# Context keys of a decoder layer: three high-and-low passes instead of plain fp32, in a new order

## The reference

```python
x = _layernorm(x + attn(x, W_Q, W_K, W_V, W_out, b_out))
# cross-attention, with xn = layer_norm(x, ln_w, ln_b) and vg the gathered context rows
q = xn @ Wq * SCALE
kv = vg @ Wkv                  # context: 77 rows of 256 -> keys 512, values 512
k, v = split(kv, 2)
sim = einsum('bthd,btkhd->bthk', q, k) + where(valid, 0, -10000)
out = einsum('bthk,btkhd->bthd', softmax(sim) * valid, v) @ Wout
# feed-forward
h = silu(x @ wg.T) * (x @ wu.T)
out = h @ wd.T
```

## Time and profile before

| | |
|---|---|
| median of three runs | 2188.42 us (2185.69 to 2190.17) |
| the profiled execution's own time | 2187.84 us |
| its span, first to last instruction | 2186.0 us |
| mean granted TensorE clock, of full | 0.992 |
| TensorE busy | 2121.0 us, 97% |
| weight loads busy | 1864.6 us, 85% |
| VectorE, ScalarE, GpSimd busy | 1574.8, 1331.5, 393.2 us |

### The profile page before, as it was taken

The page is one execution under the profiler, slowest core; times in us unless marked ns, Lnnn a source line. Parts: engine busy times, 40 slices in busy tenths (PEclk is TensorE's granted clock), DMA queues, the critical chain, the costliest instruction groups (busy, mean ns, idle before and its releaser), DMA issues.

```text
span 2186.0 us, 55834 instructions
## 1 busy us (share of the span) xinstructions
PE 2121.0 (97%) x18368; PEld 1864.6 (85%) x18368; DVE 1574.8 (72%) x5700; ACT 1331.5 (61%) x3990; POOL 393.2 (18%) x630
## 2 busy tenths in 40 slices
PE   4899999999999999999999999999999999999986
PEld 3688888888888888888888888888888888888875
DVE  3477777777777777777777777777777777777764
ACT  5666666656666656666656666656666656666642
POOL 3211121111112111112111112111112111112111
PEclk9899999999999999999999999999999999999998
DMA  4100000000000000000000000000000000000000
GB/s 133 41 14 15 15 8 17 17 17 11 16 8 17 17 17 10 17 8 17 17 17 10 17 8 17 17 17 10 17 8 17 17 17 10 17 8 17 14 6 10
DMA packets 48599, 38.47 MB, mean 18 GB/s; under 512 B 19504, under 2 KB 46512, under 8 KB 48560
## 3 DMA queue, kind: packets, MB, share of 16 engines
q1 hardware_dynamic: 48560, 37.96, 6.1%
HBM read 29.56 MB, written 8.39 MB: 17 GB/s over the span
## 4 chain that ended last, share of the span: by engine, by line
PE 95%; DVE 1%; ACT 1%; DMA 1%; POOL 1%; issue 1%; SPq 0%; POOLq 0%; DVEq 0%; ACTq 0%
PE gen L375 21%; PE gen L377 18%; PE gen L376 18%; PE s_ps L509 10%; PE z_ps L543 7%; PE pt_ps L522 3%; PE gen L439 3%; PE gen L457 3%; PE gen L470 3%; PE z_ps L545 3%; PE pt_ps L523 3%; PE pt_ps L527 2%; PE gen L466 2%; PE gen L481 1%; PE gen L434 1%
## 5 line engine op out<-in xcount | busy, mean ns | idle before, releaser
L679 ACT ACTIVATE SM<-SM,least 128x128 f32<-128x128 f32 (+1 forms) x1024 | 452.9, 446 | 142.0 <-DVE least L975 141.9
L975 DVE CUSTOM_DVE_ANT_0 SM<-s_ps,causal 128x128 f32<-128x128 f32 (+1 forms) x1024 | 312.5, 352 | 111.3 <-PE s_ps L509 105.6
L615 ACT ACTIVATE PT<-pt_ps 128x512 f32<-128x512 f32 (+1 forms) x512 | 237.7, 485 | 207.8 <-PE pt_ps L523 161.5
L988 DVE TENSOR_SCALAR SM<-SM,total 128x128 f32<-128x128 f32 (+1 forms) x1024 | 274.5, 332 | 9.1
L1157 POOL TENSOR_TENSOR H_lo<-G,H_hi 128x256 fp32r<-128x256 f32 x192 | 142.1, 753 | 620.7 <-ACT H_hi L615 620.7
L509 PE MATMUL s_ps<-KT,QT 64*128 64x128 f32 (+1 forms) x2048 | 238.5, 351 | 4.3 <-DVE least L975 3.5
L1133 POOL TENSOR_TENSOR var<-moments,eps 128x2 f32<-128x2 f32 x96 | 18.7, 195 | 1054.3 <-DVE moments L847 1054.3
L679 ACT ACTIVATION_READ_ACCUMULATOR SM<-SM,least 128x1 f32 x1024 | 195.3, 191 | 0.0
L543 PE MATMUL z_ps<-PT,Vt 128*64 128x256 f32 x1024 | 170.4, 407 | 6.2 <-ACT PT L615 6.2
L509 PEld LDWEIGHTS s_ps<-KT,QT 64*128 64x128 f32 x2048 | 135.0, 187 | 43.2 <-issue 28.6
L984 DVE RECIPROCAL total<-total 128x4 f32<-128x4 f32 x256 | 44.4, 173 | 163.6 <-ACT SM L679 159.3
(11 more groups left out here) (176 smaller groups left out, 6611.8 us busy)
## 6 DMA issues: line engine op xcount, KB each, us to landing
xT_in<-in_xT SPq DMA_DIRECT2D x32, 256.0 KB, 2.8
x_in<-in_x SPq DMA_DIRECT2D x32, 256.0 KB, 2.8
out<-XN SPq DMA_DIRECT2D x32, 256.0 KB, 2.2
ctx_in<-in_ctxT SPq DMA_DIRECT2D x32, 77.0 KB, 2.4
mask_in<-in_maskT SPq DMA_DIRECT2D x32, 77.0 KB, 2.6
QX<-in_wq SPq DMA_DIRECT2D x1, 512.0 KB, 4.6
QP<-in_wq SPq DMA_DIRECT2D x1, 512.0 KB, 5.4
xwk<-in_xwkv SPq DMA_DIRECT2D x1, 512.0 KB, 5.5
```

The costliest lines, as they stand in the source:

```text
L615: return act.activation(o, i, ACT.Copy)
L679: ins = act.activation(part, part, ACT.Exp, scale=-1.0, bias=least[:, i % 2, n:n + 1], accum_out=total[:, i % 2, n:n + 1])
L975: ins = dve.tensor_tensor_reduce(SM[:, i % 2, at:at + keys], s_ps[h][:, t * P:t * P + keys], causal[:, S - keys:S], -SCALE, -3 * NEG, ALU. ...
L988: ins = dve.tensor_scalar(part, part, total[:, i % 2, n:n + 1], None, ALU.mult)
```

## The change

The weights of the context keys become a pair of halves, `xwk_s`, staged like the others and so the first late weight after the out projection; there are 12 late weights in place of 11. The context halves get a 78th column, set to zero once by GpSimd, and the keys are computed by `project` from the halves, 78 columns wide, in 8 blocks of three passes. Of each 78 columns ScalarE copies 77 as before. The keys now wait for `ctx_low` and not for the landing of `ctx_in`, and the next context's transfer waits for `ctx_low` alone. The scratch of dynamic DMAs is set to 4096 bytes. The order of all four engines is written anew.

```diff
-        xwk = sb("xwk", [P, KD, XE])
+        xwk_s = halves("xwk", [P, KD, XE])
...
-        ctx_s = halves("ctxs", [P, KD, V])
+        ctx_s = halves("ctxs", [P, KD, V + 1])
...
-        for w, parts, per in ((wq, wq_s, 1), (wk, wk_s, 2), (wv, wv_s, 2), (wo, wo_s, 4), (xwkv[:, XE:], xwv_s, 2),
+        for w, parts, per in ((wq, wq_s, 1), (wk, wk_s, 2), (wv, wv_s, 2), (wo, wo_s, 4), (xwkv[:, 0:XE], xwk_s, 2),
+                              (xwkv[:, XE:], xwv_s, 2),
...
                     if it.other:
-                        for bank, value in it.read("oXK"):
-                            sp.wait_ge(gen_read[bank], value)
                         sp.wait_ge(ctx_low.sem, ctx_low.at(b, 0))
...
-                    sp.dma_start(xwk[:, :, :], xwkv[:, 0:XE].rearrange("(k p) n -> p k n", p=P)).then_inc(small_in.sem, 16)
...
                     elif kind == "XK":
-                        pe.wait_ge(ctx_loaded.sem, ctx_loaded.at(r, 1))
+                        pe.wait_ge(ctx_low.sem, ctx_low.at(r, 1))
                         for m in range(XP):
-                            for k in range(KD):
-                                ins = pe.matmul(ps[:, m * V:(m + 1) * V], xwk[:, k, m * P:(m + 1) * P],
-                                                ctx_in[:, k, :], start=(k == 0), stop=(k == KD - 1))
+                            ins = project(ps[:, m * (V + 1):(m + 1) * (V + 1)], tile_of(xwk_s, slice(m * P, (m + 1) * P)),
+                                          tile_of(ctx_s, whole), KD)
...
-                fill("oXK")
+                fill("aQ1")
                 scores(0)
-                fill("aQ1")
+                fill("aK1")
...
                 fill("aQ3")
+                transposed("a", 4)
+                values("a", 3)
                 fill("oSIM10")
-                values("a", 3)
                 scores(6)
-                transposed("a", 4)
...
-                        copy(KX[:, :, :], ps[:, 0:XP * V].rearrange("p (m v) -> p m v", m=XP)).then_inc(read_out, 1)
+                        copy(KX[:, :, :], ps[:, 0:XP * (V + 1)].rearrange("p (m v) -> p m v", m=XP)[:, :, 0:V]).then_inc(read_out, 1)
...
                 gated_low(4)
-                gated_low(5)
                 late()
                 x_low()
+                gated_low(5)
...
+            for part in ctx_s:
+
+                pool.memset(part[:, :, V:V + 1].bitcast(F32), 0.0).then_inc(pool_set.sem, 1)
```

More of the change, by code:

```diff
@@ L554, in body @@
                 values("o", 7)
+                fill("aV1")
                 scores(1)
-                fill("aV0")
[L557 to L563, removed]
+                fill("aQ2")
+                fill("oOUT0")
+                fill("fT3")
+                fill("oOUT1")
+                fill("fFFN0")
+                transposed("a", 0)
+                scores(2)
+                fill("aV0")
                 fill("fFFN1")
-                fill("aK1")
+                fill("oXK")
+                transposed("a", 1)
                 scores(3)
[L567 to L570, removed]
                 fill("oT10")
                 fill("oT11")
+                values("a", 0)
+                fill("fFFN2")
+                scores(4)
                 transposed("a", 2)
-                scores(4)
                 fill("fFFN3")
@@ L585, in body @@
                 fill("aQ3")
+                transposed("a", 4)
+                values("a", 3)
                 fill("oSIM10")
[L587 removed]
                 scores(6)
[L589 to L590 removed]
                 fill("oXV")
                 transposed("a", 5)
+                fill("fDOWN0")
                 values("a", 4)
[L594 removed]
+                fill("fDOWN1")
+                values("a", 5)
                 scores(7)
[L596 removed]
                 fill("oT200")
                 fill("oT201")
[L599 to L601 removed]
+                fill("nQ0")
+                fill("nK0")
                 fill("oT210")
                 fill("oT211")
+                transposed("a", 6)
                 fill("oXPV0")
@@ L734, in body @@
                 probs_out("o", 7, 0)
-                split_context()
+                fill("aQ1")
+                probs_out("o", 7, 1)
+                fill("aK1")
                 late(0)
                 exps(0, 0)
-                probs_out("o", 7, 1)
-                fill("oXK")
                 z_high_out("o", 3)
-                fill("aQ1")
+                split_context()
+                fill("aV1")
+                fill("aQ2")
                 exps(0, 1)
@@ L744, in body @@
                 exps(1, 0)
+                fill("fT3")
+                exps(1, 1)
+                fill("fFFN0")
                 fill("aV0")
-                exps(1, 1)
                 probs_out("a", 0, 0)
-                fill("fT3")
+                fill("fFFN1")
                 probs_out("a", 0, 1)
-                fill("aV1")
                 late(2)
                 exps(2, 0)
+                fill("oXK")
+                gated_high(0)
                 exps(2, 1)
[L754 to L757, removed]
-                fill("fFFN2")
[L759 to L764, removed]
+                fill("oT11")
+                gated_high(1)
+                probs_out("a", 1, 0)
+                probs_out("a", 1, 1)
+                fill("oT10")
+                fill("fFFN2")
+                nx_high_out()
                 late(3)
                 exps(3, 0)
-                fill("oT11")
+                gated_high(2)
+                exps(3, 1)
                 fill("fFFN3")
[L769 to L776, removed]
                 late(4)
                 exps(4, 0)
+                gated_high(3)
+                fill("fFFN4")
+                probs_out("a", 2, 0)
                 exps(4, 1)
+                probs_out("a", 2, 1)
+                fill("fFFN5")
                 fill("oXQ0")
+                z_high_out("a", 0)
+                gated_high(4)
                 fill("oXQ1")
@@ L1095, in body @@
                 context_shift(0)
+                probabilities(5)
+                fill("oSIM10")
                 fill("oSIM11")
-                fill("oSIM10")
-                probabilities(5)
+                masked(6, 0)
                 z_low_out("a", 1)
-                masked(6, 0)
-                fill("fDOWN1")
+                context_shift(1)
                 masked(6, 1)
                 context_probs(0)
-                context_shift(1)
+                fill("fDOWN0")
+                fill("fDOWN1")
+                context_probs(1)
                 probabilities(6)
-                context_probs(1)
-                fill("fDOWN0")
+                z_low_out("a", 2)
+                masked(7, 0)
+                masked(7, 1)
                 moments_3()
-                masked(7, 0)
-                z_low_out("a", 2)
                 fill("oXPV0")
-                masked(7, 1)
-                y()
-                fill("oXPV1")
-                probabilities(7)
+                probabilities(7)
+                fill("oXPV1")
+                y()
                 for chain, batch in ((mask_steps, r), (sx_steps, r), (gate_steps, f)):
```

76 lines of the change are left out of this document (38 added, 38 removed), and 6 rows, old and new, of the table ITEMS.

## The result

The changed kernel took 2208.87 us (median of 4 runs, 2207.95 to 2210.8) against 2189.3 us for the kernel before (4 runs, 2185.69 to 2191.41): a ratio of 1.0092, 95% interval 1.0075 to 1.011. It is slower by 0.9%, 19.6 us. The prediction was slower, 2217 us, in a range of 2203 to 2235.

What follows compares the result with a forecast made beforehand. TensorE's own passes were taken to bound the kernel: +0.93 for keys and -0.12 for order make +0.81 us per iteration, +25.9 over 32 batches; with +2.8 at the start, +28.7, so 2217 us, range 2203 to 2235.

Steps and rivals of the forecast that it cites:

- What bounds the kernel: Whole kernel: TensorE busy 97% of the span and 65.70 of 65.70 us per loop iteration, so hiding waits there wins nothing.
- The keys' passes: Context keys: 24 passes replace 16 weight loads, each at the load's pace of 0.116 us: +0.93 us per iteration.
- The rivals by columns: Context keys: 0.036 us a pass if columns pace, 2156 us, chance 0.08; 0.134 at fp32's column price, 2231, chance 0.10.
- the first rival: Context keys: columns set the pace, 0.036 us a pass, giving 2156 us; chance 0.08.
- The order: TensorE's loop: 29 runs of one kind of work, not 30, about 0.1 us per switch; -0.12 us per iteration taken.
- The waits in the loop: TensorE's loop: nothing added by new waits; the rival of about 1 us in every iteration gave 2246 us, chance 0.05.
- the three places: XK, fDOWN0 and oT200, whose inputs come sooner after their producer: covered by more than 10, 2.8 and 2.7 us.
- The first iteration: Start of the kernel: late staging +4.0 us and the removed direct transfer -1.2, together +2.8 us.
- the twelfth weight: First iteration: the keys' weights staged as one more late weight cost +4.0 us, between 0 and 8.
- the direct transfer: First iteration: the 512 KB direct transfer leaving the crowd at the start gives -1.2 us, between -2 and 0.
- The ends: First and last iterations: +0.81 us counted over all 32 batches, up to 2 us perhaps swallowed by waits of the last iterations.

## Why the prediction came out as it did

**What bounds the kernel: right.** TensorE fills the iteration before and after, and nothing that other engines do shows in the loop.

**The keys' passes: right, and shown.** I put the three passes at +0.93 us per iteration, from eight more loads at 0.116; it is +0.92 (changed order with and without them), from eight at 0.112 and 0.02 at the edges. At the keys' place in the old order it would have been 0.72; the forecast had no term for the neighbours of the keys' form. That the weight load and not the columns is the pace was an inference from the slope of the load records and from narrow plain fp32; two experiments that changed one of the two sizes each (96 weight columns, 128 context columns) bear it out, and two that changed the number or the form of the passes. The rivals by columns are refuted: neither 0.036 nor 0.134 us per pass is there. The Trainium skill's figure for a weight load ("TensorE: Matmul & The Clock Gate", LDWEIGHTS: columns over 1.2 GHz, so 107 ns for 128 and 80 ns for 96) agrees with the measured 112 and 85 less 5 ns. The 35 ns for 78 columns, which I read in the same page of the Trainium skill (section "Back-to-back issue gap") as a voice for the first rival, was misread: the section calls its formula that of an isolated matmul, which at few columns counts no weight load. Its figure for a stream of pairs with 128 columns, about 81 ns, isn't met here: passes of 128 columns stood 0.11 us apart.

**The order: mis-sized.** This is the step of the sum that failed: I took -0.12 us per iteration, and it is -0.31 (65.39 for 65.70, with plain keys in both). I had counted one switch between array halves less at 0.1 us; the run with the switch put back gives 0.19. The other 0.12 no run isolates, but the starts in the traces say where it lies. The same 16 records take 0.20 us less up to the next work (1052.06 to 1054.00 in the earlier trace rows, 1006.51 to 1008.25): 0.10 on entering, since their second record starts 0.07 after the first and not 0.17, and 0.09 on leaving, since transposes and not scores follow. The queries `aQ1`, now at the head behind values, pay 0.09 of it back, 1.61 us for 1.52, here from its first pass to scores(0) in the changed kernel and to the transposes before:

```profile
1064.41 0.39 PE L373 MATMUL gen<-xTs_hi,wq_hi 128*128 128x256 f32 x1
...
1066.02 0.93 PE L506 MATMUL s_ps<-KT,QT 64*128 64x128 f32 x8
```

```profile
1054.86 0.39 PE L375 MATMUL gen<-xTs_hi,wq_hi 128*128 128x256 f32 x1
...
1056.37 0.27 PE L522 MATMUL pt_ps<-ident,SM 128*128 128x128 f32 x1
```

I had seen the entry in the earlier trace rows, priced it at 0.05, and let the queries pay all of it; the exit I had not priced. Other pieces with new neighbours gained and lost up to 0.2 us each and nearly cancel. Over the loop the order makes 29 x 0.19 = 5.5 us of the 9.2 by which the sum was too high (28.7 forecast, 19.5 between the spans); most of the rest is in the ends, below. The keys' move had opened 0.86 us of waits and slower entries, and the new order closed it; before and after differ in the net alone.

**The waits in the loop: right.** At the three places that I worked out, none appeared. A fourth I did not look at: scores(0), which the keys at the head had covered. In the new order `aQ1` stands there.

**The first iteration: near in size, wrong in cause.** Forecast +2.8, and measured +2.9 to the second scores(0), which is luck. Of its two terms, the twelfth weight (+4.0) isn't borne out: in the old order 12 weights took 0.2 to 1.8 us longer than 11. Nor is the direct transfer (-1.2): the first scores(0) came at 24.13, 23.78, 24.19 and 23.32 us with the transfer at the start and between 23.43 and 24.63 without. The new order costs the first iteration 4.8 us, where a copy on ScalarE went behind late weights, and I did not look at its places on ScalarE for this iteration; 1.94 us of keys that left the stretch hide a part of it.

**The ends.** I let all 32 iterations grow by 0.81, so +2.4 us outside the 29; measured are +0.63 in the second and -1.62 in the tail, -1.0 together. The tail scatters from 144.5 to 150.3 us over the traces of the new order, whatever the keys' form. TensorE idles there, its granted clock drops to the 1.2 GHz level in one or another stretch, and the length goes with how much: mean granted clock 0.97 in the tail of 144.5 us, 0.96 in 144.9 (the changed kernel), 0.94 to 0.95 in 145.4 to 147.7, 0.93 in 149.0 and 0.92 in 150.3. (The prediction saw the lower level in the first slices only; the earlier trace rows has 0.91 in the last stretch.) So -1.62 in one profile is no effect of the change that I can claim.

## What to carry to other kernels

Where a matmul is narrow, count weight loads, not columns: by these runs a split into three passes could pay only where the plain form is paced by columns, which no run here had; plain fp32 with 77 columns already ran at the pace of its 16 loads. Look for this in the loads' own rows (their length against their count of columns, and the distance from one to the next) before splitting. And price the moves that a change forces on its own: a position at the head of an iteration can cover a wait that no profile of the old kernel shows.

## What the runs showed of the hardware

- A load of 128x128 weights sets 0.112 us per pass, for high-and-low passes of 78 and of 128 columns and for plain fp32 records of 77 alike; a load of 128x96 sets 0.085, for high-and-low passes of 78 and plain records of 77. A second load of the same weights is as dear as the first.
- Putting column-half work between two pieces of row-half work costs 0.19 us (one run).
- 16 plain fp32 records take 1.74 us up to transposes, 1.90 up to a projection in halves and 1.94 from values to scores.
- Kernels of the new order differ in the tail by 6 us, with a mean granted clock from 0.97 to 0.92 there, while within a trace the loop's iterations repeat to 0.03 us.
